# A scan kernel's sigmoid steps: GpSimd's inverse ahead of the low half, two weight tiles a step later, unit 0 cleared in step 10

## What is computed

```python
ek = exp(min(k, 30)); ekv = ek * k
nf, df = forward scans  a = a * decay + ekv,  b = b * decay + ek
nb, db = the same, backward
euk = exp(min(u + k, 30))
num = nf + nb - ekv + euk * k
den = df + db - ek + euk
y = sigmoid(x) * num / max(den, 1e-8) * (0.8 + 0.2 * tf)
out = x + y @ binarized(weight).T + bias
```

## Time and profile before

| what | value |
|---|---|
| median of three runs | 514.49 us |
| profiled execution, its own time | 513.52 us |
| its span, first to last instruction | 511.5 us |
| VectorE busy | 94% of the span |
| ScalarE busy | 81% |
| GpSimd busy | 74% |
| TensorE, matmuls | 352.3 us, 69% |
| mean granted TensorE clock | 0.870 of 2.4 GHz |

### The profile page before, as it was taken

One profiled execution on the slowest core, in us unless ns is written; L12 is line 12 of the kernel. 1 busy time (PEld: TensorE's weight loads), 2 busy tenths in 40 slices (PEclk: granted clock), 3 DMA queues, 4 the chain that ended last, 5 costly groups with the idle time before them and its releaser, 6 DMA issues.

```text
span 511.5 us, 5395 instructions
## 1 busy us (share of the span) xinstructions
PE 352.3 (69%) x1797; PEld 206.7 (40%) x1803; DVE 482.0 (94%) x346; ACT 413.9 (81%) x461; POOL 380.3 (74%) x210
## 2 busy tenths in 40 slices
PE   3323223332194877878597879869739999999996
PEld 2213223332152444335354445535425555544442
DVE  6999999999999699999999999999999999999566
ACT  3979899899979889988987989998797888894500
POOL 0067778748764987789788687889897799899483
PEclk9997666565678798898987989989987999999999
DMA  8878999999987498798979869989792679975379
GB/s 219 220 220 267 263 260 243 307 297 251 246 191 179 68 240 182 163 199 189 195 170 160 201 130 203 197 178 202 162 162 49 118 124 157 178 127 80 42 107 223
DMA packets 101283, 94.22 MB, mean 184 GB/s; under 512 B 2924, under 2 KB 93064, under 8 KB 100744
## 3 DMA queue, kind: packets, MB, share of 16 engines
q0 software_dynamic: 31440, 36.18, 46.9%
q1 hardware_dynamic: 67720, 56.65, 35.7%
q10 hardware_dynamic: 2096, 1.05, 0.8%
HBM read 60.31 MB, written 37.75 MB: 192 GB/s over the span
## 4 chain that ended last, share of the span: by engine, by line
POOL 27%; ACT 25%; PE 21%; issue 18%; DVE 7%; DMA 0%; SPq 0%; ACTq 0%; DVEq 0%; POOLq 0%
POOL wkv L379 11%; PE prod L447 8%; POOL acts L342 5%; POOL out_dram L355 4%; ACT x_nat L801 4%; POOL wkv L385 3%; ACT euk L659 3%; PE prod L488 3%; ACT terms L655 3%; ACT L806 3%; POOL terms L388 2%; ACT L801 2%; ACT rec L690 2%; PE sT L488 2%; PE kT L488 2%
## 5 line engine op out<-in xcount | busy, mean ns | idle before, releaser
L447 PE MATMUL prod<-acts,sgn 128*128 128x512 f16 x752 | 182.7, 399 | 0.0
L925 DVE TENSOR_TENSOR_SCAN terms<-cols,y_start,terms 128x1024 f32<-128x1024 f32 x64 | 147.0, 2337 | 1.1
L911 DVE TENSOR_TENSOR_SCAN terms<-cols,terms 128x1024 f32<-128x1024 f32 x64 | 142.8, 2272 | 0.0
L362 POOL TENSOR_TENSOR wkv<-wkv,terms 128x1024 f32<-128x1024 f32 x31 | 73.5, 2370 | 54.8 <-DVE wkv L954 54.8
L447 PEld LDWEIGHTS prod<-acts,sgn 128*128 128x128 f16 x752 | 77.2, 103 | 88.5 <-issue 16.7
L379 POOL TENSOR_TENSOR wkv<-euk,rec 128x1024 f32<-128x1024 f32 x31 | 82.1, 2648 | 33.2 <-ACT rec L692 33.1
L342 POOL TENSOR_TENSOR acts<-wkv,rec 128x1024 f16<-128x1024 f32 x30 | 78.4, 2612 | 5.0 <-ACT rec L701 4.9
L385 POOL TENSOR_TENSOR wkv<-wkv,rec 128x1024 f32<-128x1024 f32 x31 | 79.6, 2569 | 1.2 <-ACT wkv L753 1.2
L422 PE MATMUL prod<-ident,o_nat 128*128 128x128 f16 x64 | 8.3, 311 | 72.0 <-ACT o_nat L794 72.0
L422 PE MATMUL sT<-ident,x_nat 128*128 128x128 f32 x208 | 36.7, 334 | 27.5 <-ACT x_nat L801 11.2
L422 PE MATMUL kT<-ident,k_nat 128*128 128x128 f32 x248 | 43.4, 333 | 15.9 <-DVE own L942 15.8
(11 more groups left out here) (120 smaller groups left out, 585.7 us busy)
## 6 DMA issues: line engine op xcount, KB each, us to landing
terms<-own POOLq DMA_DIRECT2D x32, 512.0 KB, 5.2
out_dram<-in_x_dram SPq DMA_DIRECT2D x32, 512.0 KB, 7.2
k_nat<-in_fside_BxSxS_dram SPq DMA_DIRECT2D x30, 512.0 KB, 6.4
x_nat<-in_x_dram SPq DMA_DIRECT2D x26, 512.0 KB, 4.9
out_dram<-o_nat POOLq DMA_DIRECT2D x24, 512.0 KB, 8.4
y_fm<-in_L_ffn_weight_dram SPq DMA_DIRECT2D x8, 512.0 KB, 8.4
out_dram<-in_L_ffn_bias_dram POOLq DMA_DIRECT2D x8, 512.0 KB, 6.6
x_end<-in_x_dram SPq DMA_DIRECT2D x6, 512.0 KB, 8.7
```

The lines of the kernel that those rows point to most:

```text
L362: pool.tensor_tensor(wkv[n % 2][:, :], wkv[n % 2][:, :], ekv[n % NV], ALU.mult).then_inc(st["base"], 1)
L447: ins = pe.matmul(made_in(u), view[:, c, m % CT * P:m % CT * P + P], acts[:, part, m // CT % 2 * CT + c, h * H:(h + 1) * H], start=(part = ...
L911: dve.tensor_tensor_scan(buf, d, buf, 0.0, ALU.mult, ALU.add).then_inc(st["F" + kind], 1)
L925: dve.tensor_tensor_scan(buf[:, ::-1], d, buf[:, ::-1], y_start[:, i:i + 1], ALU.mult, ALU.add)\
```

## The change

Three helpers name the steps. `turns(n)`: step n has a sigmoid set (0, 3, 6, 8, 9, 12, 15, 18, 21, 24). `hurried(n)`: the step behind one (4, 7, 9, 10, 13, 16, 19, 22). `put_off(n)`: steps 3 and 6.

- GpSimd, in a hurried step: the low half leaves its place between the check and the inverse; it stands behind the numerator's DMA and waits for den(n). In the step behind a hurried one the store moves from ahead of the check to the end of the step.
- ScalarE: `hasty` becomes hurried(n), which adds step 9. In steps 11, 14, 17, 20 and 23 (`ahead`) the first clear stands ahead of the inverse. Abs and Sign of tiles 3 and 6 move to the next step, behind two; the copy of the turned tile goes behind exps there.
- TensorE: the turns of weight tiles 3 and 6 move to the next step, behind the turn of k.
- The planner: cleared(9) becomes 0, it was 1.

```diff
+    CLEARED = {9: 0, 23: 32, 25: 35, 26: 38, 27: 41, 28: 44, 29: 47}
...
+    def turns(n):
+        return n < SOON and (n % 3 == 0 or n == CT)
+    def hurried(n):
+        return 2 <= n < LAST and turns(n - 1)
+    def put_off(n):
+        return 0 < n < CT and turns(n)
...
-                if n < N - 1:
+                if n < N - 1 and not hurried(n - 1):
                     for m in ready[0:1]:
                         store(m)
                     ready = ready[1:]
...
-                if low:
+                if low and not hurried(n):
                     low_half(n - 2, p)
...
                 pool.dma_start(ekv[n % NV], own[p][:, :], accum_op=ALU.add).then_inc(num_in[p], 16)
+                if hurried(n):
+                    done(pool, "den", n)
+                    low_half(n - 2, p)
...
+                if put_off(n - 1):
+                    w_turn(n - 1, 1 - p)
...
-                if wt:
-                    done(pe, "sgn", n)
-                    done(pe, "wTc", n - 1)
-                    turn(lambda c: wT[:, c, :], CT, lambda c: s_nat[p][:, c * P:(c + 1) * P],
-                         ident16[:, :]).then_inc(st["wT"], 1)
+                if wt and not put_off(n):
+                    w_turn(n, p)
...
+                sooner = cleared(n - 1) if n == LAST + 2 else min(made(n - 1), cleared(n - 1) + 1)
+                ahead = hurried(n - 1) and not hurried(n) and LAG < n < LAST
+                if ahead:
+                    clear(cleared(n - 1), sooner)
                 if mid:
                     inverse(n - 1, 1 - p)
...
-                hasty = low and n < LAST and n % 3 == 1
+                hasty = hurried(n)
...
-                if late and n < N - 2 and not hasty:
+                if late and n < N - 2 and not hasty and not ahead:
                     clear(cleared(n - 1), sooner)
...
-                if 1 <= n <= CT:
-                    done(act, "wT", n - 1)
-                    act.mul(sgn[:, :, (n - 1) * P:n * P], wT, SIGN).then_inc(st["wTc"], 1)
+                if put_off(n - 1):
+                    signs(n - 1, 1 - p)
+                elif 1 <= n <= CT:
+                    turned_signs(n - 1)
...
-                if wt:
...
+                if put_off(n - 1):
+                    turned_signs(n - 1)
+                if wt and not put_off(n):
+                    signs(n, p)
```

More of the change, by code:

```diff
@@ L64, in made @@
         return 0 if n < LAG else 2 * LAST if n > N - 4 else MORE.get(n, 2 * (n - LAG + 1))
-    CLEARED = {23: 32, 25: 35, 26: 38, 27: 41, 28: 44, 29: 47}
+    CLEARED = {9: 0, 23: 32, 25: 35, 26: 38, 27: 41, 28: 44, 29: 47}
     def cleared(n):
@@ L440, in s_turn, with w_turn @@
                      ident[:, :]).then_inc(st["sT"], 1)
+            def w_turn(n, p):
+                done(pe, "sgn", n)
+                done(pe, "wTc", n - 1)
+                turn(lambda c: wT[:, c, :], CT, lambda c: s_nat[p][:, c * P:(c + 1) * P],
+                     ident16[:, :]).then_inc(st["wT"], 1)
             def product(u, tiles):
@@ L701, in halves, with signs, turned_signs @@
                 act.mul(rec[p][:, :], high, LO_GAIN).then_inc(st["hib"], 1)
+            def signs(n, p):
+                landed(act, w_in, n, p)
+                done(act, "abs", n - 1)
+                act.activation(junk, w_nat[p][:, :], ACT.Abs, accum_out=asum[:, n:n + 1])\
+                   .then_inc(st["abs"], 1)
+                done(act, "wT", n - 2)
+                act.activation(s_nat[p], w_nat[p][:, :], ACT.Sign, scale=TINY_GAIN, bias=tiny[:, 0:1])\
+                   .then_inc(st["sgn"], 1)
+            def turned_signs(n):
+                done(act, "wT", n)
+                act.mul(sgn[:, :, n * P:(n + 1) * P], wT, SIGN).then_inc(st["wTc"], 1)
             def early_out(i):
@@ L734, in step @@
                     halves(n - 2, p)
-                sooner = cleared(n - 1) if n == LAST + 2 else min(made(n - 1), cleared(n - 1) + 1)
                 if not wt and not late:
@@ L785, in step @@
                         clear(sooner, later)
-                if wt:
[L788 to L796, removed]
+                if put_off(n - 1):
+                    turned_signs(n - 1)
+                if wt and not put_off(n):
+                    signs(n, p)
+                if turns(n):
                     if n % 3 == 0:
```

## The result

The changed kernel takes 518.66 us in the median of four runs (517.72 to 519.79), the kernel before 513.73, now also of four (511.86 to 514.51). The ratio is 1.0102 with an interval of 1.0065 to 1.0139: it is slower by 4.9 us, and the interval excludes no change. The execution profiled took 519.79, 6.3 over the profiled one of before; it is the slowest of the four.

What follows compares the result with a forecast made beforehand. The prediction took VectorE, busy 482.0 of 511.5 us, and how its 32 steps follow one another as the bound. Terms -3.7 + 5.2 - 0.3 + 2.5 + 0.8 = +4.5 on 513.5 gave 518.0 us, range 510 to 521.5.

Steps and rivals of the forecast that it cites:

- Steps 3 to 9: Late weights and GpSimd's new order bring the inverse forward, so the denominator of step 9 starts earlier: -3.7 us.
- Steps 9 to 11: Turn of k behind clear(0), and clear(3) ahead of Ln, make the gate of step 11 late: 5.2 us lost, to +1.5.
- Rival (b): TensorE at 2.4 GHz in step 10, its turns ending sooner: -1.9, so +2.6 and 516 us; chance 0.15.
- Steps 12 to 17: Order saves in steps 13 and 16; step 17's clear, waiting for its product, gives step 16's saving back: to +1.2 us.
- back at 1.23 (13 perhaps 2): Sign that the forecast is right: denominators of steps 4, 7, 13 and 16 last 1.23 us, 13 perhaps 2.
- Step 20: Clear of unit 22, ahead of Ln, waits for its product and makes the gate late: +2.5 us, to +3.7.
- Steps 21 to 23: Inverse 0.3 late in step 21, 1.1 saved in 22, lost at a product in 23: +0.8 us, to +4.5.
- Rival (a): The clearing ahead of Ln costs nothing and the order does what it says: -4 to -6, 508.5 us; chance 0.17.
- (c): Gains and losses cancel: clearings of steps 17, 20 and 23 hidden with TensorE at 2.4 GHz: 514 us; chance 0.18.
- (d): The inverse overlaps the denominator as before and only losses are left: 525 us; chance counted with (e).
- (e): GpSimd falls behind at the next base; inverse late in steps 12, 15, 18, +1 each: 521 us; 0.10 with (d).
- The price of taking turns: In step 11, a GpSimd operation that lets a denominator in first lasts 1.0 longer by the row, 1.2 by exclusive lock.

Runs made afterwards that it cites:

- e4: The kernel before with only the weights' lines of the change (tiles 3 and 6 put off): 509.86 us, ratio 0.9958 to before.
- e9: The changed kernel without any clear ahead of Ln and with weight tiles 3 and 6 in their old steps: 510.48 us, ratio 0.9965 to before.
- e2: The changed kernel with TensorE's turn of unit 0 moved to step 10, behind the turns of x and k: 517.44 us, ratio 1.0083 to before.
- e1: The changed kernel with the first clear back behind Ln and Exp in steps 11, 14, 17, 20 and 23: 507.26 us, ratio 0.9906 to before.
- e10: The changed kernel once more, unaltered, for a second trace: 518.35 us in two runs, ratio 1.0113 to before.
- e7: The changed kernel with the clear ahead of Ln in step 20 alone: 511.40 us, ratio 0.9982 to before.
- e6: The kernel with e1's and e2's edits, without GpSimd's wait for the denominator ahead of the low half: 509.84 us, ratio 0.9953 to before.

## Why the prediction was right, and where its steps were off

The forecast was 518.0 in the time of the profiled execution, and 519 against the median shown. The measured median is 518.66, a ratio of 1.0102 where 518.0 to 513.5 is 1.009. The mechanism held: the gains up to step 10, the turn of k behind unit 0, and the clear ahead of Ln that waits for a product. That the number came out so closely is in part luck, since errors of 0.9 to 1.6 us in steps 14, 17, 20 and 23, all where a product took longer or shorter than I had assumed, had different signs.

- *Steps 3 to 9, -3.7.* Measured: -3.5. The stretches of steps 4 and 7 went, 0.17 (0.35 expected) came back in step 5 and 0.65 (0.4) in step 8. e4 and e9 confirm the two parts.
- *Steps 9 to 11, +5.2, to +1.5.* The gate of step 11 stands at +1.83. The links were as worked out: clear(0) ended at 161.8 (161.5), k was turned at 166.4 (166.2), val began at 169.92 (169.5), the check at 178.73 (178.4). Ln of step 10 came at 155.39; its sum, 160.68 - 2.5 - 2.9, makes 155.3 and not 155.1 to 155.2. e2 shows the turn's share, e1 that of the clear ahead of Ln. Rival (b) fell: the clock between 162 and 167 was 0.50. What (b) had for it, that no idle time this long was in the trace, was a misreading, at least as to the length: in the trace of before a weight tile's turn at 80.44 came behind 11.92 of idle time, and those of x and k right behind it took 1.92 each, at clock 0.50 between 81.2 and 83.5.
- *Steps 12 to 17, to +1.2.* Measured: +2.1. Two terms were wrong in size and nearly cancelled: step 14, which I gave nothing, lost 1.3, and step 17, which I had lose its 1.1, lost nothing. I had taken each product's length from the trace of before, 3.62 for unit 9 and 5.30 for unit 15. They came out as 5.30 and 3.62, because TensorE's idle time ahead of them had changed places too: 1.90 became 3.61, and 3.66 became 2.08. Step 13 saved 0.4, and its denominator still lasts 2.88, so my sign "back at 1.23 (13 perhaps 2)" did not come there; nor did ScalarE wait ahead of the clear in step 17. The turn and the product of unit 9, before and after (the product after is shown under e10):

```profile
211.55 0.63 PE L422 MATMUL yT<-ident,y_fm 128*128 128x128 f32 x4 [1.90 <-ACT o_nat L678]
212.02 3.62 PE L447 MATMUL prod<-acts,sgn 128*128 128x512 f16 x16
```

```profile
214.50 0.63 PE L435 MATMUL yT<-ident,y_fm 128*128 128x128 f32 x4 [3.61 <-ACT o_nat L696]
```

- *Step 20, to +3.7.* The gate stands at +3.64, which is luck. I counted the step from step 19's check, at +1.2, and gave it 2.5. The check of step 19 came at 294.69, +2.1, and from there to the gate the kernel lost 1.6. The missing 0.9 is TensorE's clock again: the product of unit 21, ahead of unit 22, took 3.62 behind 0.65 of idle time, where it had taken 4.53 behind 3.64. One link was otherwise too: the denominator got the port between low half and inverse, not ahead of the low half. e7 shows the price of this clear alone.
- *Steps 21 to 23, to +4.5.* Measured: +6.4. The three steps cost 2.7, not 0.8. Step 22 saved 0.5 instead of 1.1, and step 23 lost 2.7 instead of 1.1, as its product took 5.99. In e10's trace step 23 lost 1.3, but step 14 more. From step 24 to 30 VectorE kept its pace but for 0.2 lost in step 25 and 0.8 gained in step 27 (whose stretch I had put down to step 26), and 0.9 was lost behind step 30. The profiled execution is therefore 1.8 over my sum, the median 0.7.
- *Rival (a)*, faster (508.5), supposed that the clears ahead of Ln cost nothing. It fell, and e1 without them shows 507.26. Its chance stands as 0.17 in one place and 0.18 in another. *(c)* had the clearings hidden where the products run at full clock. That came true in step 17 alone: in step 20 the products of units 21 and 22 ran at clock 1.00, and clear(22) still waited 2.86. *(d)* fell with e9. *(e)* had steps 12, 15 and 18 lose 1 each; 15 and 18 lost nothing, and 12 lost 0.4.
- *The price of taking turns.* The inverse beside a denominator lasted 3.33 in step 20 (2.35 + 1.0), so the row's 1.0 held rather than the whole 1.2 that I worked out from the Trainium skill, page "SBUF — State Buffer", section "SBUF: two separate sides", where the engine that comes second "fully blocks". That the one who begins first keeps the other out for its whole instruction, e6 bears out: 0.28 of a lead cost 2.25.

## What to carry to other kernels

An operation that is moved ahead on an engine to fill a wait brings its own wait along. Ask what it waits for, and whether that is ready when the old wait begins; here it wasn't in four of five steps. Where an operation's clearing goes to a later step, look through the other engines' queues for what stands behind its next use, as the turn of k did behind unit 0. And with two engines that take turns at a port, who begins first decides: a wait that the data don't need, as the low half's for the denominator, can be worth 0.75%.

## What the runs showed of the hardware that I had not expected

How long one and the same product takes went with TensorE's idle time ahead of it. For units 9, 15, 21 and 29 the twelve traces give 48 products of 16 matmuls of 128x512, each behind one turn with one idle time in front. The 20 behind 0.65 to 2.88 of idle time took 3.62 each, at a granted clock of 1.00. The 28 behind 2.93 to 4.74 took 4.53 to 6.19, at a mean granted clock of 0.58 to 0.80; among these a longer idle time did not always mean a longer product (6.19 behind 3.67, 5.04 behind 4.74). I had read these lengths as properties of the units. A change that moves about 1 us of idle time on TensorE can make them 0.9 to 2.6 longer or shorter, and ScalarE's clear behind them with it.

The last idle time is not the whole account, though. The product of unit 25 in the changed kernel's two traces, with the turn ahead of it:

```profile
319.45 0.63 PE L435 MATMUL yT<-ident,y_fm 128*128 128x128 f32 x4 [2.03 <-ACT o_nat L696]
319.91 3.62 PE L467 MATMUL prod<-acts,sgn 128*128 128x512 f16 x16
```

```profile
321.12 0.63 PE L435 MATMUL yT<-ident,y_fm 128*128 128x128 f32 x4 [2.02 <-ACT o_nat L696]
321.59 5.30 PE L467 MATMUL prod<-acts,sgn 128*128 128x512 f16 x16
```

The program and the idle time are the same, and the lengths differ by 1.7. What decides there, these runs don't show.

How VectorE and GpSimd take turns, on the other hand, was regular. The twelve traces have 126 denominators up to step 30 that began while an operation of GpSimd with two SBUF inputs was running and that lasted 1.3 or more. Each ended 1.07 to 1.10 after that operation. In 16 of them the next such operation stood right behind in GpSimd's queue. The denominator still came between the two, and the row of that next operation shows 3.32 to 3.35 instead of 2.35. The one exception is step 4 of the kernel before: its denominator began at 75.32, the inverse at 75.33, with the low half ending at 75.38, and it was the denominator that waited, until 1.08 after the inverse.
